# A four-layer graph network with expert layers on one core: sparse routers that work on raw rows, and moved pieces at the start of two block loops

## The chip, the core and the metric

One core of a Trainium2 chip runs the whole program in one launch. The metric is the device time in microseconds (us). The kernel before takes 1663.86 us, the median of 3 runs (1663.5 to 1666.35).

## What is computed

Rows x (625 nodes by 512 features, f32) go through eight steps, each `x = x + step(layernorm(x))`: four graph layers (GNN) and, after each, a layer of 8 experts. In layers 1 and 3 the expert layer is sparse: each row goes to its two best experts alone.

```python
x = x + _L1_ffn_ref(_layernorm(x, axis=-1)[None], gate_w, gate_b, w1, b1, w2, b2)[0]

# layer 1                                          # layer 3
logits = x @ gate_w + gate_b                       logits = x @ router_w.T
topk_vals, topk_idx = top_k(logits, 2)             probs = softmax(logits)
weights = softmax(topk_vals), one-hot to experts   gates, idx = top_k(probs, 2); gates = gates / sum(gates)
h = relu(x @ w1[e] + b1[e])                        h = silu(x @ w1[e].T) * (x @ wgate[e].T)
out = sum_e (h @ w2[e] + b2[e]) * weights[:, e]    out = sum_e combine[:, e] * (h @ w2[e].T)
```

The layer norm has no gains: `(x - mean) / sqrt(var + 1e-5)`. The expert layers 0 and 2 are dense (every expert for every row).

## The kernel before, in words

**Layout.** The 625 rows lie in 5 tiles of 125 rows (`X`, T = 5). `XN` is the normalised copy, `XT` its transpose (512 features in 4 groups of 128 partitions by 625 rows). Each engine has its own program in the file (PE's begins near L768, ACT's near L1500, DVE's near L1935, POOL's near L585, SP's near L555); they meet through semaphores, and each engine goes through its own list strictly in order. So what stands where in a list is the schedule.

**The sparse layer.** A router r (1 or 3) finds for each row two experts. The rows are counted per expert, each expert's rows get whole blocks of 128 slots, 17 blocks in all, and PE works through the blocks. For each block it needs the 128 rows turned (`xblk`, then `xbh` and `xbl`, a rounded value and the rest) and the weights of the block's expert, in a rounded part ("high", written by ACT, L1627) and a rest ("low", written by DVE, L384). Each product is three passes: high by high (L1075), rest by high (L1076), high by rest (L1079).

**Router before, as each engine runs it.** DVE: `normalise` writes XN (L2003), `feats` copies the transposes to XT (L1950), `low` makes the first weights' rest (L384), then `router(r)` (L2106 to L2159): logits, maximum, exp (ACT L1568), sum, quotient `PR`, the 8 sorted values and indices (L2135, L2138), the mask `MK` of the two chosen (L2146), and the weights `COMB` (L2152 to L2159). PE: `routed_feats` turns XN (L779), multiplies XT by the gate matrix (L800, 16 instructions), waits for ACT's copy of the logits, turns them into rows (L958). `slots` on PE (L1039) counts the mask with 12 narrow products and waits for COMB; `slots` on DVE (L2183 to L2205) gives the slot of each row and the two-hot tiles `SEL0`. With `SEL0` PE picks the first block's rows in 40 products (`chosen_nodes`, L1116), so that block 0 needs no transfer; POOL meanwhile scatters all rows of XN to DRAM (`scatter`, L688) for the later blocks.

**Start of the block loop before (`block_loop`, `body1`).** In layer 1 PE turns COMB (L1056), adds the second biases of rows 0 and 1 (L1061, 4 instructions) ahead of block 0's nodes, then runs the first product of block 0, the other biases (L1053), the second product, block 1's nodes by `SEL1` (L1116 again), and `turn(0)` (L1101). DVE at this place: xbl (L2268), the rest of weights a1, `blocks_of` (which expert has which block, L2213 to L2225, on which SP waits for the loads of block 1; then the kept weights and block biases, L2228 to L2237), `second_rows` (SEL1, L2242 to L2248), `second_biases` (L2256), the hidden copy (L2280), the rest of weights y0, and xbl of block 1 (L2268).

**keep(b, n)** is n products of constants (L790, two instructions each) whose result nobody reads; they occupy PE while it would wait.

## Time and profile before

| | us |
|---|---|
| median of 3 runs | 1663.86 |
| the profiled execution | 1662.77, span 1660.0 |
| PE busy | 1586.0 (96%) |
| DVE busy | 1243.7 (75%) |
| ACT busy | 935.0 (56%) |
| POOL busy | 292.2 (18%) |
| mean granted TensorE clock | 0.987 of full |

The page gives each engine's busy time, the span in 40 slices of 41.5 us, the chain of work that ended last, and the costliest groups of instructions. PE is on 79% of that chain and DVE on 14%. The two routers lie at 686 to 734 us and 1159 to 1205 us; the block loops behind them run to about 945 and 1645 us.

### The profile page before, as it was taken

What the parts mean: (1) busy time and instruction counts of PE and PEld (TensorE: products, weight loads), DVE (VectorE), ACT (ScalarE), POOL (GpSimd) and SP (SyncE); (2) the same over time, 40 slices, a digit from 0 to 9 for tenths busy, and PEclk for the clock granted to TensorE, in tenths of its full rate; (3) what the DMA queues carried; (4) which work ended last, traced back from release to release, by engine and by line L of the source; (5) the groups of instructions that cost most, each with busy time, mean ns of one, the idle gap of its engine ahead of it and who ended that gap; (6) DMA issues with size and microseconds to landing.
All of it is one profiled execution on the core that took longest, in us unless ns stands there. A gap on an engine that the chain in (4) does not pass through costs nothing.

```text
span 1660.0 us, 26245 instructions
## 1 busy us (share of the span) xinstructions
PE 1586.0 (96%) x8681; PEld 1243.7 (75%) x8681; DVE 1243.7 (75%) x2138; ACT 935.0 (56%) x1572; POOL 292.2 (18%) x276
## 2 busy tenths in 40 slices
PE   9997998999999999889999999999899999999998
PEld 8885765868877886477788765865588888888886
DVE  8836663464756575879999868553799999999997
ACT  1423463443634462249999653421388787787884
POOL 0023730010210121179000302000470000000003
PEclk9998999999999999989999999999999999999999
DMA  8010000022001002054952340005253438935003
GB/s 337 20 46 6 1 2 14 1 115 77 2 3 37 1 2 102 26 171 151 325 207 93 89 159 1 1 1 228 54 221 138 169 127 358 387 141 219 25 19 99
DMA packets 42239, 173.14 MB, mean 104 GB/s; under 512 B 10219, under 2 KB 10472, under 8 KB 26681
## 3 DMA queue, kind: packets, MB, share of 16 engines
q1 hardware_dynamic: 28742, 153.75, 24.2%
q0 software_dynamic: 8960, 10.29, 2.3%
q10 hardware_dynamic: 4464, 8.13, 1.3%
q8 instruction: 46, 0.75, 0.2%
q14 instruction: 27, 0.22, 0.0%
HBM read 275.54 MB, written 19.25 MB: 178 GB/s over the span
## 4 chain that ended last, share of the span: by engine, by line
PE 79%; DVE 14%; issue 2%; ACT 2%; POOL 1%; DMA 1%; DVEq 0%; SPq 0%; ACTq 0%; POOLq 0%
PE bank L1075 10%; PE bank L1079 10%; PE bank L1076 10%; PE bank L927 4%; PE bank L899 4%; PE bank L974 3%; PE bank L887 3%; PE bank L839 3%; PE bank L1023 3%; PE bank L1199 3%; PE bank L1307 3%; PE bank L858 2%; PE bank L1369 2%; PE bank L1101 2%; PE bank L1281 2%
## 5 line engine op out<-in xcount | busy, mean ns | idle before, releaser
L715 POOL DMA_INDIRECT sb_W<-slots_out,sb_slus x20 | 29.9, 1494 | 541.3 <-DMA slots_out<-sb_rC 535.8
L1530 ACT ACTIVATE sb_rF<-sb_rF,sb_nmx 125x625 f32<-125x625 f32 (+4 forms) x120 | 89.5, 746 | 45.0 <-DVE sb_nmx L2072 44.9
L653 POOL TENSOR_TENSOR sb_rstd<-sb_ve,sb_half 125x3 f32<-125x3 f32 (+4 forms) x29 | 25.4, 876 | 442.7 <-DVE sb_ve L1976 238.1
L790 PE MATMUL bank<-sb_ones 128*128 128x512 f32 x208 | 95.5, 606 | 3.8 <-DVE sb_rC L2625 1.3
L384 DVE TENSOR_TENSOR sb_rA_r<-sb_W,sb_rA_r 128x1024 fp32r<-128x1024 f32 x68 | 83.6, 1229 | 12.2 <-ACT sb_rA_r L1627 12.0
L2072 DVE CUSTOM_DVE_ANT_0 sb_rF<-bank,sb_rG 125x625 f32<-125x625 f32 x80 | 61.5, 807 | 36.1 <-PE bank L887 35.2
L384 DVE TENSOR_TENSOR sb_XT_r<-sb_W,sb_XT_r 128x1024 fp32r<-128x1024 f32 x68 | 83.3, 1226 | 0.0
L384 DVE TENSOR_TENSOR sb_rB_r<-sb_W,sb_rB_r 128x1024 fp32r<-128x1024 f32 x68 | 83.2, 1224 | 0.0
L1627 ACT ACTIVATE sb_rA_r<-sb_W 128x1024 fp32r<-128x1024 f32 x68 | 71.5, 1052 | 19.5 <-DMA sb_W<-in_w_m 15.8
L1662 ACT ACTIVATE sb_rG_r<-bank 128x512 fp32r<-128x512 f32 x51 | 30.6, 600 | 82.3 <-PE bank L1101 82.3
L790 PEld LDWEIGHTS bank<-sb_ones 128*128 128x128 f32 x208 | 39.0, 193 | 47.9 <-issue 44.5
L927 PE MATMUL bank<-sb_rA,sb_rDE 125*64 125x125 f32 x1040 | 69.0, 275 | 4.5 <-DVE sb_rA L2086 4.3
L899 PE MATMUL bank<-sb_ident,sb_rF 125*125 125x125 f32 x520 | 69.7, 279 | 3.0 <-DVE sb_nmx L2072 3.0
L1627 ACT ACTIVATE sb_XT_r<-sb_W 128x1024 fp32r<-128x1024 f32 x68 | 71.6, 1053 | 0.0
L1627 ACT ACTIVATE sb_rG_r<-sb_W 128x1024 fp32r<-128x1024 f32 x68 | 71.6, 1053 | 0.0
L1627 ACT ACTIVATE sb_rB_r<-sb_W 128x1024 fp32r<-128x1024 f32 x68 | 71.3, 1049 | 0.3 <-PE bank L1079 0.3
L927 PEld LDWEIGHTS bank<-sb_rA,sb_rDE 125*64 125x64 f32 x1040 | 54.8, 136 | 20.6 <-DVE sb_rA L2086 13.0
L899 PEld LDWEIGHTS bank<-sb_ident,sb_rF 125*125 125x125 f32 x520 | 61.3, 188 | 9.0 <-issue 6.8
L384 DVE TENSOR_TENSOR sb_AT_r<-sb_W,sb_rG_r 128x1024 fp32r<-128x1024 f32 x51 | 62.0, 1216 | 0.0
L2086 DVE COPY sb_rA<-bank 125x500 f32<-125x500 f32 (+3 forms) x60 | 37.6, 627 | 30.7 <-PE bank L899 30.6
L1075 PE MATMUL bank<-sb_XT_r,sb_rC_r 128*128 128x512 f32 x136 | 59.3, 436 | 0.0
L1075 PE MATMUL bank<-sb_rA_r,sb_rC_r 128*128 128x512 f32 x136 | 53.6, 394 | 4.4 <-ACT sb_rC_r L1641 3.9
(534 smaller groups left out, 4783.5 us busy)
## 6 DMA issues: line engine op xcount, KB each, us to landing
sb_W<-in_w_m SPq DMA_DIRECT2D x204, 1024.0 KB
sb_rDE<-in_w_m SPq DMA_DIRECT2D x17, 1024.0 KB
sb_rC<-slots_in SPq DMA_DIRECT2D x33, 256.0 KB, 2.7
sb_W<-in_w_g SPq DMA_DIRECT2D x8, 1024.0 KB, 4.9
slots_out<-sb_rC ACTq DMA_DIRECT2D x31, 256.0 KB, 2.0
slots_in<-sb_rC SPq DMA_DIRECT2D x1, 4608.0 KB, 24.7
sb_W<-in_w_a SPq DMA_DIRECT2D x4, 1024.0 KB, 17.1
sb_W<-in_w_m SPq DMA_DIRECT2D x2, 2048.0 KB, 16.8
```

The source lines that it names most:

```text
L384: eng.tensor_tensor(lo, src[:, HALF * h:HALF * (h + 1)], hi.bitcast(F32), ALU.subtract).then_inc(split(r, p, h, b, "lo")[0], 1)
L790: pe.matmul(bank[:, b, :], ones[:], ones[:, 0:1].broadcast_to([P, D]), start=True, stop=True)
L839: mm = pe.matmul(bank[:, j, 0:hi - lo], w[:, c, m * P:(m + 1) * P], x[:, c, lo:hi], start=(n == 0), stop=(n == len(steps) - 1))
L887: mm = pe.matmul(bank[0:R, b, at:at + n], q[hp, h // 2, t * R:(t + 1) * R], keys, start=(i == 0), stop=(i == len(terms) - 1))
L899: return pe.transpose(bank[0:R, b, at:at + R], SM[:, (2 * p + a) % 4, kb * R:(kb + 1) * R], ident[0:R, 0:R])
L927: mm = pe.matmul(bank[a * DH:(a + 1) * DH, 6 + g % 2, p % 2 * R:(p % 2 + 1) * R], V[:, kb, h + a, :], PT[:, p % 2, 8 + a if kb == 4 else 4 ...
L1075: pe.matmul(dst, high[2 * h + k], w_hi[:, k], start=(opens and h == 0 and k == 0), stop=False)
L1076: pe.matmul(dst, low[2 * h + k], w_hi[:, k], start=False, stop=False)
L1079: mm = pe.matmul(dst, high[2 * h + k], w_lo[:, k], start=False, stop=(closes and h == 1 and k == 1))
L1530: act.activation(SM[:, s % 4, 0:kn], SM[:, s % 4, 0:kn], ACT.Exp, scale=-1.0, bias=nmx[:, s:s + 1], accum_out=dens[:, s:s + 1]).then_inc(S ...
L1627: act.activation(half(r, p, h)[0], part(PLACE[r][p])[:, HALF * h:HALF * (h + 1)], ACT.Copy).then_inc(split(r, p, h, b, "hi")[0], 1)
L2072: dve.tensor_tensor_reduce(out=SM[:, s % 4, 0:kn], in0=scores, in1=mask(t), scale=-1.0, scalar=3e38, op0=ALU.add, op1=ALU.min, accum_out=n ...
```

## The change

- **Router on raw rows.** `raw_gates` turns the raw rows X as soon as each tile is final, ACT copies each tile to XT (`raw_tiles`), and PE multiplies the tile by the gate columns straight into rows. `picks` on DVE corrects for the mean (mean times the gate columns' sum, `gsum`) and multiplies by 1/sqrt(var). The 8 sorted values come from the logits; the mask MK is done before exp and the weights, and PE's `slots` waits for the mask alone. `gsum` is made once, inside router 0: 8 narrow products on PE and one copy on DVE.
- **XN** is written by ACT (`normal_rows`), after the mask.
- **Fewer constant products.** keep(7, 17) becomes keep(7, 10) ahead of router 1, keep(7, 6) ahead of router 3 goes, the routers' keep(5, 4) becomes keep(5, 3), and two keep(5, 3) stand around `slots` and the turning of COMB in layer 1.
- **Moved pieces.** COMB is turned in `turn_weights`, ahead of the block loop; biases 0 and 1 come after block 0's nodes; the nodes of block 0 go tile by tile as SEL0 is written; block 1's nodes come ahead of the product a1; `second_rows` comes ahead of the rest of a1 on DVE; the rest of weights a0 comes after `slots`; `blocks_of` runs ahead of the block loop, and the kept weights and block biases become `kept_weights` at the old place.

```diff
+            def raw_gates(r, ready, base):
+                for t in range(T + 1):
+                    if t < T:
+                        pe.wait_ge(ready, base + t + 1)
+                        for c in range(C):
+                            mm = pe.transpose(bank[:, t, c * R:(c + 1) * R], X[:, t, c * P:(c + 1) * P], ident[0:R, 0:R])
+                        mm.then_inc(S("tr_full"), 1)
+                    if t >= 1:
+                        u = t - 1
+                        pe.wait_ge(S("x0"), ROWS_XT[r] + u + 1)
+                        for c in range(C):
+                            mm = pe.matmul(bank[0:R, 7, u * E:(u + 1) * E], XT[:, c, u * R:(u + 1) * R], gw[:, c, GW[r]:GW[r] + E],
+                                           start=(c == 0), stop=(c == C - 1))
+                mm.then_inc(S("rt_pe"), 1)
...
-                pe.wait_ge(S("rt_vec"), ROUTED[r] + ROUTER_OPS[r])
+                pe.wait_ge(S("rt_vec"), ROUTED[r] + PICKED[r])
...
+                if c == 3:
+                    for k in range(C):
+                        pe.matmul(bank[0:R, 2, 0:32], ones[:, 0:R], gw[:, k, 0:32], start=(k == 0), stop=(k == C - 1))
...
-            keep(7, 17)
-            routed_feats(4, 5, 1)
-            feats_ready(5)
+            keep(7, 10)
+            raw_gates(1, S("lf_vec"), LF_OPS)
+            keep(5, 3)
             slots(1)
-            second_biases(0, 2)
+            turn_weights()
+            keep(5, 3)
             block_loop(1)
...
-            keep(7, 6)
-            routed_feats(8, 9, 3)
-            feats_ready(9)
+            raw_gates(3, S("rows_vec"), 3 * T)
+            keep(5, 3)
             slots(3)
             keep(5, 4)
             block_loop(3)
...
                         second_biases(2, T)
-                        first("a", 1, b)
                         pe.wait_ge(S("rows_off"), 2 * T + 1)
                         pe.wait_ge(S("b_xbl"), 1)
                         chosen_nodes(lambda t: SEL1[t])
+                        first("a", 1, b)
...
-                pe.wait_ge(S("sl_vec"), SLOT_OPS * (r // 2) + SELECTED)
-                chosen_nodes(lambda t: SEL0[:, t])
+                pe.wait_ge(S("x0"), ROWS_XN[r] + T)
+                chosen_nodes(lambda t: SEL0[:, t], True)
+                if r == 1:
+                    pe.wait_ge(S("rt_act"), RT_ACT[1] + 3)
+                    pe.wait_ge(S("ld_b2"), 64)
+                    second_biases(0, 2)
...
+            def raw_tiles(r):
+                for t in range(T):
+                    act.wait_ge(S("tr_full"), T * (5 if r == 1 else 9) + t + 1)
+                    act.activation(XT[:, :, t * R:(t + 1) * R], bank[:, t, 0:C * R]..., ACT.Copy).then_inc(S("x0"), 1)
+            def normal_rows(r):
+                act.wait_ge(S("ln_vec"), LN[4 if r == 1 else 8] + STATS + 1)
+                for t in range(T):
+                    act.activation(XN[:, t], X[:, t], ACT.Identity, scale=rstd[...], bias=shift0[...]).then_inc(S("x0"), 1)
...
+            def picks(r):
+                c(dve.tensor_tensor(EX[:], means, gsum[...], ALU.mult))
+                dve.wait_ge(S("rt_pe"), RT_PE[r] + 1)
+                c(dve.tensor_tensor(LG[:], bank[0:R, 7, 0:T * E]..., EX[:], ALU.subtract))
+                dve.wait_ge(S("pow"), POW[f"ln{k}"])
+                c(dve.tensor_tensor(LG[:], LG[:], bcast(rstd[0:R, :], E), ALU.mult))
+                dve.scalar_tensor_tensor(out=shift0[:], ...).then_inc(S("ln_vec"), 1)
+                if r == 1:
+                    c(dve.tensor_tensor(LG[:], LG[:], rbias[...], ALU.add))
+                for t in range(T): c(dve.max(m8[:, t], LG[:, t]))
+                for t in range(T): c(dve.max_index(i8[:, t], m8[:, t], LG[:, t]))
+                c(dve.tensor_copy(if8[:], i8[:]))
+                for k in range(2):
+                    c(dve.tensor_tensor(EQ[:, k], iota8..., if8[:, :, k:k + 1]..., ALU.is_equal))
+                c(dve.tensor_tensor(MK[:], EQ[:, 0], EQ[:, 1], ALU.add))
+                assert c.n == ROUTED[r] + PICKED[r]
+                c(dve.tensor_tensor(LG[:], LG[:], m8[:, :, 0:1]..., ALU.subtract))
+                dve.wait_ge(S("rt_act"), RT_ACT[r] + 1)
+                c(dve.tensor_tensor(COMB[:], EX[:], MK[:], ALU.mult))
+                c(dve.tensor_reduce(red[:, 2], COMB[:], AX.X, ALU.add))
+                c(dve.reciprocal(red[:, 2], red[:, 2]))
+                c(dve.tensor_tensor(COMB[:], COMB[:], bcast(red[:, 2], E), ALU.mult))
...
-            normalise(n, 4, X)
-            feats(5, XT)
+            picks(1)
+            slots(1)
             low(dve, 1, ("a", 0), 0, part(PLACE[1]["a", 0]))
-            router(1)
-            slots(1)
+            blocks_of(1)
...
-                    lows(("a", 1), b)
                     if before is None:
-                        blocks_of(1)
                         second_rows()
+                    lows(("a", 1), b)
+                    if before is None:
+                        kept_weights(1)
                         second_biases()
```

## Rows read from the trace of the kernel before

**Rows 1.** The page's part 2: granted TensorE clock in tenths, 40 slices.
```profile
PEclk9998999999999999989999999999999999999999
```
**Rows 2.** Chain that ended last, layer 1's router: start, duration, engine, output, line, count.
```profile
683.41 0.65 DVE sb_X L2661
...
699.63 1.48 PE bank L1039 x12
...
702.47 3.77 PE bank L1061 x4
...
706.24 7.59 PE bank L1116 x40
```
**Rows 3.** PE's timeline there: start, duration, line; in brackets idle before and releaser.
```profile
670.26 14.82 PE L790 MATMUL bank<-sb_ones 128*128 128x512 f32 x34
...
686.24 2.47 PE L779 MATMUL bank<-sb_ident,sb_XN 125*128 125x125 f32 x20 [1.16 <-DVE sb_XN L2003]
...
715.27 0.47 PE L1075 MATMUL bank<-sb_rA_r,sb_rC_r 128*128 128x512 f32 x1 [1.46 <-ACT sb_rC_r L1641]
...
718.20 2.83 PE L1053 MATMUL bank<-sb_b,sb_rF 8*125 8x512 f32 x6
...
725.80 1.97 PE L1116 MATMUL bank<-sb_rA,sb_XN 125*128 125x128 f32 x8 [1.80 <-DVE sb_rB L2248]
...
733.62 0.47 PE L1075 MATMUL bank<-sb_rA_r,sb_rC_r 128*128 128x512 f32 x1 [1.02 <-ACT sb_rC_r L1641]
```
**Rows 4.** DVE's timeline, the same stretch.
```profile
696.51 0.44 DVE L2135 MAX8 sb_m<-sb_LG 125x8 f32<-125x8 f32 x5
...
698.37 0.20 DVE L2146 TENSOR_TENSOR sb_MK<-sb_EQ 125x40 f32<-125x40 f32 x1
...
704.31 1.40 DVE L2205 SCALAR_TENSOR_TENSOR sb_W<-sb_iotaP,sb_sl,sb_W 125x128 f32<-125x128 f32 x5
...
717.36 0.16 DVE L2213 TENSOR_TENSOR sb_nblk<-sb_nblk 128x8 f32<-128x8 f32 x1
...
719.05 0.24 DVE L2228 TENSOR_REDUCE sb_wk<-sb_rDE 125x10 f32<-125x80 f32 x1
...
730.59 1.22 DVE L384 TENSOR_TENSOR sb_W_r<-sb_W,sb_rDE_r 128x1024 fp32r<-128x1024 f32 x1
```
**Rows 5.** Timelines of ACT, POOL and SP's queue, the same stretch.
```profile
687.38 0.59 ACT L1513 ACTIVATE sb_XT<-bank 128x500 f32<-128x500 f32 x1 [18.41 <-PE bank L779]
...
730.01 1.06 ACT L1627 ACTIVATE sb_rA_r<-sb_W 128x1024 fp32r<-128x1024 f32 x1 [13.67 <-DMA sb_W<-in_w_m]
...
704.41 1.58 POOL L688 DMA_INDIRECT slots_in<-sb_XN,sb_slu  x1 [17.67 <-issue]
...
722.24 1.18 SPq L502 DMA_DIRECT2D sb_W<-in_w_m  x2
```
**Rows 6.** Stretches: length, busy PE, PEld, DVE, ACT, POOL; granted clock, DMA share, GB/s.
```profile
703.00:706.00 3.00, 3.00 (x4) 0.65 (x2) 2.64 (x12) 1.31 (x2) 1.58 (x1) 0.50 0.01 3
...
726.00:727.00 1.00, 1.00 (x6) 1.00 (x6) 1.00 (x3) 0.00 (x0) 0.00 (x0) 0.50 0.94 393
```
**Rows 7.** PE's and DVE's timelines, layer 3's router and the block loop's start.
```profile
1164.76 0.67 DVE L2057 TENSOR_TENSOR sb_X<-bank,sb_X 125x512 f32<-125x512 f32 x1
...
1180.53 0.38 PE L1039 MATMUL bank<-sb_MK,sb_TRI 125*125 125x40 f32 x2 [1.16 <-DVE sb_COMB L2159]
...
1186.66 4.73 PE L1116 MATMUL bank<-sb_W,sb_XN 125*128 125x128 f32 x40 [1.14 <-DVE sb_W L2205]
...
1192.85 0.47 PE L1075 MATMUL bank<-sb_rA_r,sb_rC_r 128*128 128x512 f32 x1 [1.46 <-ACT sb_rC_r L1641]
...
1205.18 0.47 PE L1075 MATMUL bank<-sb_AT_r,sb_rG_r 128*128 128x512 f32 x1 [0.64 <-issue]
```
**Rows 8.** PE's timeline, router 0's logits.
```profile
275.90 4.44 PE L1347 MATMUL bank<-sb_rC,sb_gw 128*64 128x375 f32 x16
```
**Rows 9.** A stretch of the first block loop, columns as in rows 6.
```profile
740.00:750.00 10.00, 10.00 (x50) 8.21 (x49) 10.00 (x13) 9.67 (x15) 10.00 (x6) 1.00 0.45 157
```

145 lines of the change are left out of this document (84 added, 61 removed).

## Prediction

> **What bounds the kernel now.** I read four views in this order. The page's engine table and slices first: PE is busy in nearly every slice and holds a full clock nearly everywhere [rows 1], so time can only come out of places where PE waits or runs slowly. Then the chain of work that ended last around each sparse router: it leaves PE there and walks through DVE and ACT operations of 0.2 us [rows 2]. Then the timelines of PE and DVE in those two places, for the waits and what ends them [rows 3, 4, 7]. Last a stretch of the block loop behind: PE and DVE are both busy for all of 10 us [rows 9]. The loop moves as one piece, so what is saved ahead of it is kept, if DVE, ACT and the loads reach it in the old order.
>
> **Router 1 up to the mask.** Before: the last tile of X is final at 683.41 + 0.65 = 684.06 [rows 2], and the narrow counting products start at 699.63 [rows 2], 15.6 us later. After: four transposes of the last tile cost 4/20 of 2.47 = 0.49 us [rows 3]. ACT's copy of it costs 0.59 [rows 5]. The tile's logits are 8 narrow instructions; the nearest row is L1039, 12 in 1.48 us, 0.12 each [rows 2], so 0.99 a tile. Tile 3's logits stand behind tile 4's transposes and cover the copy, so the logits end at 684.06 + 0.49 + 2 x 0.99 = 686.5, with a hand-over 686.6. That assumes keep(7, 10) is over: 17 constants took 14.82 us from 670.26 [rows 3], 0.87 each, so ten end at 679.0, before the first tile.
>
> DVE then has four short operations (subtract, scale, shift0, bias), 0.23 each (0.20 for the mask's own operation [rows 4] and a hand-over), and the known piece from the first MAX8 to the mask's end, 698.57 - 696.51 = 2.06 [rows 4]. The mask is there at 686.6 + 0.92 + 2.06 = 689.6. The new keep(5, 3), 2.6 us, ends before it. The counting starts at 689.7 instead of 699.63: **9.9 us**. Exp, the sum and the weights lie beside the counting's 1.48 us.
>
> **Router 1 up to block 0's first product.** DVE's slot chain depends on the counting and shifts by 9.9. SEL0's last five operations started at 704.31 and took 1.40 [rows 4]; PE may now start at the first of the five, 704.31 + 0.28 - 9.9 = 694.7. Counting, turning and keep(5, 3) end at 689.7 + 1.5 + 0.6 + 2.6 = 694.4. The 40 products took 7.59 us here [rows 2] and 4.73 in layer 3 [rows 7]. In the first case they followed four bias products of 0.94 each [rows 2] in a stretch with a granted clock of 0.50 [rows 6]; at the full clock six such cost 2.83, 0.47 each [rows 3]. With constants ahead I take 4.73: nodes end at 699.4. The four bias instructions now follow (1.9 us) and hide the 1.46 us wait for xbh and xbl [rows 3]. Block 0's first product starts at 701.3 instead of 715.27: **14.0 us**.
>
> **From there to block 1's first product.** Before this took 733.62 - 715.27 = 18.35 us [rows 3], with PE waiting 1.80 us for SEL1 and then at half clock [rows 3, 6]. PE's new list would need 2.9 + 2.8 + 4.6 + 2.8 + 0.5 = 13.6. DVE is the later one: its old list ended with y0's rest at 730.59 + 1.22 = 731.8, 16.5 us after the first product; blocks_of, 719.05 - 717.36 = 1.7, has left it [rows 4], so 14.8. Xbl and the hand-overs are 1.46 less ACT's 0.59, 0.9 [rows 3, 5]: 15.7. So block 1 begins at 717.0 and the gain is 733.62 - 717.0 = **16.6 us**. What is late next is DVE's list; PE idles some 2 us ahead of block 1.
>
> **What is moved past other queues.** SP waits for blocks_of, which now ends near 700 instead of 719.05, so its two loads for block 1 go out near 703 instead of 722.24 [rows 5]. ACT got them at 730.01, 7.8 us later [rows 5]; that would be 711. They now share the DMA engines with POOL's ten scatters, which began at 704.41 [rows 5] and now begin near 694.5, so the loads can land as late as 714.5. ACT's two copies, xbh and xbl behind them need 3.6 us, so block 1 starts between 714.6 and 718.1: the cost is 0 to 1.1, and I take 0. Had the loads not moved, they would land at 730 and nearly all of the 2.7 us and more would be lost; this cover carries much. On ACT, the first copies of a0 end near 687.5, exp runs at 690, five XN rows at 0.59 [rows 5] end at 693.1, 1.6 us before PE wants them; if a row cost 1.06, the largest ACT piece [rows 5], it would be 0.7 late. The scatter needs XN too and is 9.9 earlier at best. On DVE the rest of a0 (2.3) and blocks_of (1.7) stand between SEL0 (695.8) and xbl (700.1): they end at 699.8, so they are free by 0.3.
>
> **Router 3.** The last X ends at 1164.76 + 0.67 = 1165.43 [rows 7]; plus 0.49 + 1.98 + 0.1 is 1168.0; three short operations and 2.06 give the mask at 1170.7, and the counting starts at 1170.8 instead of 1180.53 [rows 7]: 9.7. The nodes start at the first SEL0 tile, another 4/5 of 1.40 = 1.1 earlier. DVE has 1.7 less in the loop's first round, which should take away PE's wait of 0.64 at 1205.18 [rows 7]. Sum **11.4 us**. The 1.46 wait at 1192.85 stays [rows 7].
>
> **Router 0 pays.** gsum is 8 narrow instructions, 8 x 0.12 = 0.99, ahead of the last quarter of a group that ran without a gap (16 in 4.44 us) [rows 8], plus a DVE copy of 0.23 on the same path: **-1.2 us**. Bounds: 0 if PE was to wait there, 1.2.
>
> **The clock.** Between keep(7, 10) and keep(5, 3) PE has 7.5 us in which it does short transposes and 8-column products with gaps, in layer 3 the same for 8.3 us. The rows show what went before a half clock: narrow products with gaps at 699.6 to 702.5 went before the 0.50 of 703 to 706 [rows 2, 6], and an idle of 1.80 us before the 0.50 at 726 [rows 3, 6]. Against it, 20 transposes in 2.47 us went before a full clock [rows 3]. The change's stretches look more like the first. Price at half clock, by L1116's 7.59 against 4.73 and the biases' 0.94 against 0.47: transposes and logits +1.5, keep 2.6 more, of which 0.5 is hidden, +2.1; if it goes on, counting and turning +1.2, second keep +2.3, nodes +2.9. The bounds are 0 and 10.0 in layer 1, 0 and 9.5 in layer 3. I take the first two terms, 3.6 for each router since constants, which keep PE busy without a gap, stand right behind.
>
> The Trainium skill ("TensorE: Matmul & The Clock Gate", "What's actually happening") says that "the default state is throttled, and activity releases the throttle"; that speaks against taking constants away, and it is the second rival's rule. The same page ("Wait — 56ns, not 53.3ns?") gives about 62 ns of sequencer time for a small matmul without hardware decoding. By that, an estimate, a tile's logits would cost 0.5 and each router would come 1 us earlier, 2 in all; the narrow row here has 0.12 an instruction, and the sum goes by it.
>
> **Sum.** 16.6 + 11.4 - 1.2 = 26.8 at full clock; less 2 x 3.6 = 19.6. The profiled execution has 1662.77 (span 1660.0, 2.8 around it): 1662.77 - 19.6 = **1643.2**. The median of the runs is 1.1 above the profiled one, inside the range.
>
> **Rivals.** (1) *The clock stays full in both routers*: 1662.77 - 26.8 = 1636.0. For it: narrow work keeps PE occupied, and the 20 transposes. Against it: the half clock after 699.6 to 702.5. (2) *Half clock carries on to the nodes in both*: 26.8 - 10.0 - 9.5 = 7.3, so 1655.5. For it: the 7.59 us of the old nodes; against it: constants now stand on both sides of the counting. (3) *The change doesn't do what it says*: the mask is early, but XN or the weights of COMB end last, and only the moved pieces count, 16.6 - 9.9 + 1.7 - 1.2 = 7.2, so 1655.6. Little speaks for it; XN has 1.6 us to spare. (4) *Slower: the block loop settles in another order*. PE and DVE are both full [rows 9]; if block 1 enters with DVE late and each of the 31 later blocks (15 and 16) keeps PE waiting once for xbl, by the 1.02 us seen at 733.62 [rows 3], that is 31.6, so 1643.2 + 31.6 = 1674.8. It decides from 19.6/31 = 0.63 us a block. Against it: all but the first round's order is unchanged, and at 740 to 750 PE had no gap although 733.62 began with one.
>
> **How the numbers follow.** Forecast 0.60, rival (1) 0.18, (2) 0.12, (3) 0.04, (4) 0.04, and 0.02 that smaller losses meet at no change. Range 1634.5 to 1652.0: it takes in (1) with 1.5 for the loads and row 8's bound, and on the upper side 8.8 for a half clock that carries on in one of the two routers; it leaves out (2), (3), (4) and the rest, 0.2 at most. Faster by over 0.2% (3.3 us, about what a measurement of this kernel can tell from no change): 0.60 + 0.18 + 0.12 + 0.04 = 0.94; same 0.02; slower 0.04.
>
> **What would show it.** In the changed kernel's PE timeline: 20 narrow groups between 679 and 687 (all 1 us later for router 0), counting 15.6 - 9.9 = 5.7 us after the last X; nodes of block 0 in about 4.8 us and biases right behind; the wait ahead of block 1's first product ended by DVE's xbl, some 2 us; ACT's first copy of block 1 not later than 714.5. In layer 3 counting 5.4 us after the last X. The granted clock between each router's last X and its counting decides between the forecast, (1) and (2). The prediction is wrong if the counting is later than 8 us after the last X, if ACT's wait for block 1's load ends last, or if a block's round in either loop has become longer.

## The result, and the profile after

| | us |
|---|---|
| changed kernel, median of 5 runs | 1653.34 (1647.62 to 1655.17) |
| before, median of 5 runs beside it | 1663.86 (1661.35 to 1666.35) |
| ratio | 0.9932, 95% interval 0.9917 to 0.9946 |
| its profiled execution | 1647.62, span 1645.4, mean granted clock 0.983 |
| DVE, PE busy | 1233.9, 1580.1 |

The change gains 10.5 us. The forecast was 20.7 below the median of before and its range ended at 1652.0, so it was wrong: the sign is right, but half of the gain is missing. The profiled execution is the quickest of the five. The other four have granted clocks of 0.980 to 0.982.

PE's timeline around router 1 and the start of the first block loop (start, duration, line, tiles; in brackets the idle time before it and what ended it). It answers to [rows 3] and the PE steps of [rows 2].

```profile
687.92 0.65 PE L828 MATMUL bank<-sb_ident,sb_X 125*128 125x125 f32 x4
688.40 2.07 PE L834 MATMUL bank<-sb_gw,sb_XT 128*125 128x8 f32 x16
690.33 4.33 PE L794 MATMUL bank<-sb_ones 128*128 128x512 f32 x6
694.49 0.31 PE L1059 MATMUL bank<-sb_MK,sb_TRI 125*125 125x40 f32 x2
...
699.61 4.59 PE L1136 MATMUL bank<-sb_W,sb_XN 125*128 125x128 f32 x39 [0.59 <-DVE sb_W L2277]
...
706.15 0.50 PE L1093 MATMUL bank<-sb_rA_r,sb_rC_r 128*128 128x512 f32 x1
...
721.42 0.47 PE L1093 MATMUL bank<-sb_rA_r,sb_rC_r 128*128 128x512 f32 x1 [1.59 <-issue]
...
728.28 0.60 PE L1144 MATMUL bank<-sb_ident,sb_rC 128*128 128x128 f32 x4
...
736.64 0.49 PE L1093 MATMUL bank<-sb_rA_r,sb_rC_r 128*128 128x512 f32 x1 [1.76 <-DVE sb_rC_r L2344]
...
744.66 0.60 PE L1144 MATMUL bank<-sb_ident,sb_rC 128*128 128x128 f32 x4
```

DVE there: the last tile of X, and the mask (answers to [rows 4]).

```profile
687.12 0.75 DVE L2738 SCALAR_TENSOR_TENSOR sb_X<-sb_XN,sb_rstd,sb_X 125x512 f32<-125x512 f32 x1
...
693.14 0.20 DVE L2232 TENSOR_TENSOR sb_MK<-sb_EQ 125x40 f32<-125x40 f32 x1
```

The last X is final at 687.87, 3.8 us later than before: that much was lost upstream. From there it goes better than forecast. The counting (L1059) begins 6.6 us after the last X where before had 15.6, the nodes (L1136) run at the full clock in 4.7 (all 40), and block 1's first product (721.42) begins 33.6 us after the last X where before had 733.62 - 684.06 = 49.6 [rows 2, 3]: 16.0 us gained. Then a new loss. L1144 turns block 2's nodes at 728.28 and block 3's at 744.66. I call that distance block 2's round: 16.4 us, and 12.38 before (740.65 to 753.03). PE's wait of 1.76 us is in it, and right behind the wait a stretch at half clock, which costs some 1.7 us more (start:end, length, busy PE, PEld, DVE, ACT, POOL, then granted clock, DMA share, GB/s):

```profile
738.00:741.00 3.00, 2.92 (x7) 2.35 (x8) 3.00 (x5) 3.00 (x5) 3.00 (x2) 0.50 0.23 87
```

What the other engines did there (answers to [rows 5]): ACT's waits for DMAs, SP's DMA issues, and two of POOL's ten scatter pieces.

```profile
716.00 1.06 ACT L1670 ACTIVATE sb_rA_r<-sb_W 128x1024 fp32r<-128x1024 f32 x1 [9.16 <-DMA sb_W<-in_w_m]
724.53 1.06 ACT L1670 ACTIVATE sb_W_r<-sb_W 128x1024 fp32r<-128x1024 f32 x1 [0.85 <-DMA slots_in<-sb_XN,sb_slu]
731.18 2.02 ACT L1670 ACTIVATE sb_rDE_r<-sb_W 128x1024 fp32r<-128x1024 f32 x2 [2.94 <-DMA sb_W<-in_w_m]
```

```profile
707.73 3.60 SPq L506 DMA_DIRECT2D sb_W<-in_w_m  x2
724.52 0.34 SPq L511 DMA_DIRECT2D sb_rC<-slots_in  x1
725.15 5.58 SPq L506 DMA_DIRECT2D sb_W<-in_w_m  x4
```

```profile
708.83 2.95 POOL L692 DMA_INDIRECT slots_in<-sb_XN,sb_slu  x1 [0.30 <-issue]
...
717.59 1.19 POOL L692 DMA_INDIRECT slots_in<-sb_XN,sb_slu  x1 [0.30 <-issue]
```

Read them together. POOL's last scatter piece ends at 718.8; at 724.5 SP's and ACT's waits for the scatter end together. SP could not issue block 1's y0 load before that, since the wait and the node load (724.52) stand ahead of it on its queue. The load goes out at 725.15 and is in use at 731.18; ACT idles 2.94 us, and xbh, xbl and PE's first product of block 2 come late behind it. Before, POOL's scatter had ended 13 us ahead of block 1's first product; now it ends 2.6 ahead.

Router 3, with one line each of DVE, PE and ACT (answers to [rows 7]):

```profile
1155.81 0.68 DVE L2097 TENSOR_TENSOR sb_X<-bank,sb_X 125x512 f32<-125x512 f32 x1
```

```profile
1157.03 2.86 PE L834 MATMUL bank<-sb_gw,sb_XT 128*125 128x8 f32 x16
1159.73 5.13 PE L794 MATMUL bank<-sb_ones 128*128 128x512 f32 x6
1164.70 0.31 PE L1059 MATMUL bank<-sb_MK,sb_TRI 125*125 125x40 f32 x2
...
1169.82 4.70 PE L1136 MATMUL bank<-sb_W,sb_XN 125*128 125x128 f32 x40 [0.18 <-DVE sb_W L2277]
1175.98 0.47 PE L1093 MATMUL bank<-sb_rA_r,sb_rC_r 128*128 128x512 f32 x1 [1.46 <-ACT sb_rC_r L1684]
```

```profile
1193.87 1.06 ACT L1670 ACTIVATE sb_XN_r<-sb_W 128x1024 fp32r<-128x1024 f32 x1 [3.37 <-DMA slots_in<-sb_XN,sb_slu]
```

The counting begins 1164.70 - 1156.49 = 8.2 us after the last X (before 15.1), the first product 19.5 after it (before 27.4): 7.9 gained. The six constant passes, 2.75 us at the full clock, took 5.13. Ahead of y1's copy ACT now waits 3.37 us for the scatter; the second loop's first round (between the first two L1144) takes 28.1 instead of 26.6.

Stretches with the granted clock as third number from the end, first of the changed kernel, then of before (answers to [rows 6]):

```profile
284.00:287.00 3.00, 3.00 (x12) 2.92 (x11) 1.95 (x4) 0.75 (x2) 0.00 (x0) 0.50 0.00 0
482.00:485.00 3.00, 3.00 (x6) 1.56 (x6) 0.00 (x0) 0.00 (x0) 0.00 (x0) 0.50 0.00 0
...
1158.00:1164.00 6.00, 6.00 (x14) 3.56 (x15) 3.24 (x27) 4.33 (x6) 0.48 (x1) 0.50 0.01 1
```

```profile
284.00:287.00 3.00, 2.83 (x18) 2.54 (x17) 2.06 (x5) 1.37 (x4) 0.00 (x0) 1.00 0.03 5
292.00:295.00 3.00, 2.62 (x9) 2.65 (x10) 1.50 (x4) 2.22 (x4) 0.00 (x0) 0.58 0.00 0
482.00:485.00 3.00, 3.00 (x14) 2.33 (x13) 1.53 (x3) 0.00 (x0) 0.00 (x0) 1.00 0.00 0
```

The changed kernel has half-clock stretches (1.2 GHz instead of 2.4) where before had none, two of them far ahead of the routers. Before is not free of them: it has, among others, one at 292 to 296 us, which the changed kernel has at 294 to 298, and in router 1 two more (702 to 713 and 725 to 730). Summed over windows of 1 us, one minus the granted clock comes to 1.7 us for each, or to two or three times that. From 100 to 1640 us this makes 25.6 us in the changed kernel's trace and 20.5 in before's.

The books of the two profiled executions, as the distance of the changed kernel's PE from before's:

| place | before | after | distance |
|---|---|---|---|
| router 0's second products | 296.75 | 298.56 | +1.8 |
| turn to rows ahead of router 1 | 667.52 | 671.32 | +3.8 |
| block 1's first product, layer 1 | 733.62 | 721.42 | -12.2 |
| turn of block 2's nodes | 740.65 | 728.28 | -12.4 |
| turn of block 3's nodes | 753.03 | 744.66 | -8.4 |
| last turn of that loop | 929.95 | 919.53 | -10.4 |
| turn to rows ahead of router 3 | 1156.91 | 1147.95 | -9.0 |
| block 0's first product, layer 3 | 1192.85 | 1175.98 | -16.9 |
| turn of block 2's nodes there | 1240.60 | 1225.23 | -15.4 |
| turn of block 15's | 1586.66 | 1572.07 | -14.6 |

### The profile page after: what moved, and what is told of

It reads as the page before. It is cut to its first block, busy times and chain, and to the rows that moved or that the text cites. A ratio compares the mean times of both kernels' runs of the same rounds, so it can differ in the third digit from the quotient of the medians.

```text
span 1645.4 us, 26288 instructions
## 1 busy us (share of the span) xinstructions
PE 1580.1 (96%) x8703; PEld 1246.9 (76%) x8703; DVE 1233.9 (75%) x2122; ACT 942.8 (57%) x1584; POOL 293.5 (18%) x276
## 4 chain that ended last, share of the span: by engine, by line
PE 80%; DVE 12%; issue 3%; ACT 2%; DMA 1%; POOL 1%; DVEq 0%; SPq 0%; ACTq 0%; POOLq 0%
PE bank L1097 10%; PE bank L1093 10%; PE bank L1094 10%; PE bank L947 4%; PE bank L919 4%; PE bank L994 4%; PE bank L907 3%; PE bank L859 3%; PE bank L1043 3%; PE bank L1331 3%; PE bank L1223 3%; PE bank L878 2%; PE bank L1396 2%; PE bank L1119 2%; PE bank L1305 2%
## 5 line engine op out<-in xcount | busy, mean ns | idle before, releaser
L794 PE MATMUL bank<-sb_ones 128*128 128x512 f32 x184 | 88.5, 628 | 3.8 <-DVE sb_rC L2702 1.3
L1670 ACT ACTIVATE sb_XT_r<-sb_W 128x1024 fp32r<-128x1024 f32 x68 | 71.7, 1055 | 0.0
L1670 ACT ACTIVATE sb_rB_r<-sb_W 128x1024 fp32r<-128x1024 f32 x68 | 71.4, 1050 | 0.2 <-PE bank L1097 0.2
## 6 DMA issues: line engine op xcount, KB each, us to landing
sb_W<-in_w_m SPq DMA_DIRECT2D x2, 2048.0 KB, 16.9
```

Source lines behind the costliest of these rows:

```text
L794: pe.matmul(bank[:, b, :], ones[:], ones[:, 0:1].broadcast_to([P, D]), start=True, stop=True)
L1670: act.activation(half(r, p, h)[0], part(PLACE[r][p])[:, HALF * h:HALF * (h + 1)], ACT.Copy).then_inc(split(r, p, h, b, "hi")[0], 1)
```

## Experiments

The theory that I formed from these traces (S): the routers' part of the forecast holds; the missing gain is in the scatter, which has become late, in the sums' place in router 0, and in half-clock stretches.

**The changed kernel again.** No edit.

> The changed kernel again, unchanged. Theory S (the scatter of the first routed layer has become late, and half-clock stretches fall at other places each time): 1651 to 1655 us as a median, and the executions stay some 7 us apart with the granted clock (0.980 to 0.983). In its trace block 2 of the first loop again takes 16.4 us after block 1 where before had 12.4, and the first round of the second loop 28.1 where before had 26.6, while the half-clock stretches of the middle of the kernel need not be where they were. Rival L (a late load was an accident of the one profiled execution): block 2's round is 12.4 to 12.9 and the median comes out near 1650.

Measured: 1653.24 us (1649.31 to 1654.51), ratio 0.9928 (0.9912 to 0.9944). Block 2's round is 14.8 us, again with ACT waiting for y0 (2.49 us); the second loop's first round is 27.2. The difference to 16.4 is the half clock behind PE's wait, which this trace lacks:

```profile
738.00:741.00 3.00, 2.56 (x13) 1.87 (x12) 3.00 (x4) 3.00 (x5) 3.00 (x2) 1.00 0.23 87
```

The loss is a property of the kernel, its size is not: theory S holds with smaller numbers, rival L falls. In router 3 the half clock lies at 1158 to 1169 us and costs 5.1 instead of 3.4.

**Before, again.** No edit.

> The kernel before, unchanged, for a second trace of it. Question: are the half-clock stretches that only the changed kernel's four traces have ahead of its first routed layer (284 to 288 us in all of them, 481 to 486 in three) a property of the change or of the execution? Theory C (the stretches fall by chance; any kernel may get them): this trace has one at 284 to 288 us or at 481 to 486 us too, or its landmarks ahead of router 1 lie 1 to 3 us from those of the first trace of before. Theory P (the change brings them, in router 0 by the sums of the gate weights and the order around them): no such stretch, the start of router 0's second products at 296.5 to 297.0 us and the turn to rows ahead of router 1 at 667.5 within 0.5 us.

Measured: 1663.92 us, ratio 0.9998 (0.9985 to 1.0011). Ahead of router 1 its stretches are those of the first trace of before and the turn to rows is at 668.04, 0.5 later: P. Router 0's second products start at 297.23, outside the range expected, but 20.9 us after the logits' start (276.37) as in the first trace. Behind it two more stretches came (1050 to 1055 and 1170 to 1174 us) and its end lies 3.9 us behind the first trace's, so far down one kernel differs from itself by whole microseconds.

**The y0 load ahead of the scatter's wait.**

```
                 weights(("a", 1), 1, e, new)
+                weights(("y", 0), 1, e, new)
                 sp.wait_ge(S("sc"), 16 * 2 * T * (r // 2 + 1))
                 nodes(2)
-                weights(("y", 0), 1, e, new)
```

> The changed kernel with one load moved on SP's queue: the y0 weights of block 1 of the first loop go ahead of SP's wait for the scatter and of the node load of block 2, which were ahead of them. Theory S: VectorE is done with these weights' place at 720.7 us, the scatter's wait kept SP until 724.5, and the load landed at 731.2 with ScalarE idle 2.9 us for it; issued at 721 it lands by 728, ScalarE's wait of 2.9 us goes, VectorE's 1.5 and TensorE's 1.8 after it too, and block 2's round falls from 16.4 to 12.4 to 13.6 us. The median falls by 2 to 4 us to 1650 (half clock at 737 to 741 us, which followed TensorE's pause, may go as well). Rival D (the load is slow because the scatter's packets share the DMA engines, not because it is issued late): it lands at 730 or later all the same and the round stays above 15 us, the median within 1 us of the changed kernel's.

Measured: 1651.88 us (ratio 0.9923, 0.9908 to 0.9938). SP's issues and PE's turns of nodes:

```profile
708.84 13.52 SPq L506 DMA_DIRECT2D sb_W<-in_w_m  x3
725.62 0.34 SPq L511 DMA_DIRECT2D sb_rC<-slots_in  x1
```

```profile
730.09 0.66 PE L1144 MATMUL bank<-sb_ident,sb_rC 128*128 128x128 f32 x4 [0.60 <-DMA sb_rC<-slots_in]
...
742.55 0.60 PE L1144 MATMUL bank<-sb_ident,sb_rC 128*128 128x128 f32 x4
```

Three loads are out by 722.4 instead of two, ACT waits no more for y0, and block 2's round is 12.46, with block 1's first product 33.6 us after the last X as in the changed kernel: the mechanism is as theory S said, and rival D falls. Now PE waits 0.60 us for the node load. The median moved by 1.4 us, less than the 2 to 4 expected and within what the intervals leave open. Over the whole loop, from block 2's turn to the last turn, this trace takes 190.0 us, and the two of the changed kernel 191.3 and 192.8 (before 189.3): there the edit is worth 1.2 and 2.8.

**Half the scatter.** The rows of each node's second expert are not scattered, and who waits for the scatter waits for that half.

```
-                for k in range(2):
+                for k in range(1):
                     for t in range(T):
                         pool.indirect_dma_start(out=XS, ...
```

> The changed kernel with only half of each scatter: the first expert's rows of each token go to the slots, those of the second are left out (5 of 10 indirect DMAs), and who waits for the scatter waits for that half. Theory S: POOL is done near 709 instead of 718.8 us, no wait of SP or ScalarE ends with the scatter; block 2's round in the first loop 12.4 to 13.4 us instead of 16.4, the second loop's first round 26.6 to 27.0 instead of 28.1; the median 4 to 6 us under the changed kernel's, 1647 to 1649. Rival O (the first rounds are longer because of the new order of nodes, products and blocks ahead of the loop): both rounds stay, and the median stays within 1.5 us.

Measured: 1649.25 us, ratio 0.9904 (0.9887 to 0.9921), 4.1 below the changed kernel. No wait of ACT or SP ends with the scatter; block 2's round 12.7, the second loop's first round 26.7. Taken alone this trace doesn't show that the scatter is the cause, for half clock in router 1 (688 to 695 and 711 to 719 us) made block 1's first product late, 38.0 us after the last X instead of 33.6. With the full scatter and as late a start (two constants, below: 37.9) the rounds are 12.4 and 26.7 as well, and with the sums left out (36.3) block 2's is 12.5. A block that starts that much later no longer waits for the load. And rival O falls by these traces, which have the new order and rounds as short as before's.

**The moved pieces alone.** The kernel before, with the moved pieces (turned copy, biases, nodes by tile, SEL1 ahead, blocks counted ahead), the keep(5, 3) ahead of block 0's nodes, and its own routers.

> The kernel before with the moved pieces alone: turned copy of the weights and biases 0 and 1 at their new places, block 0's nodes tile by tile, block 1's nodes ahead of the second part of block 0's first products, blocks counted ahead of the loop; the routers stay on normalised rows. By the forecast's terms: router 1 gives 14.0 - 9.9 = 4.1 us to block 0's first product and 16.6 - 14.0 = 2.6 more to block 1's, router 3 10.8 - 9.7 = 1.1 and its wait of 0.64; together 8.4, so 1655 to 1657 us against a median of 1664 to 1666 of before. Theory S (the lateness of the scatter, which ran to 720 us in before, is met only where all parts come together): block 2's round in the first loop stays at 12.4 to 13. Rival O (the new order itself makes block 2's round longer): it is 14 us or more, and the gain only 4 to 6 us. Theory N on the 0.06 us that every round of the second loop lost: if a moved piece brings it, the rounds are 26.68 here, otherwise 26.62.

Measured: 1656.27 us, ratio 0.9959 (0.9945 to 0.9973), 7.5 us gained. Block 0's nodes and block 1's first product:

```profile
704.66 4.73 PE L1115 MATMUL bank<-sb_W,sb_XN 125*128 125x128 f32 x40 [0.48 <-DVE sb_W L2208]
...
726.49 0.47 PE L1072 MATMUL bank<-sb_rA_r,sb_rC_r 128*128 128x512 f32 x1 [1.58 <-issue]
```

Block 0's first product comes 4.0 us earlier (forecast 4.1), block 1's 7.1 (forecast 6.7), router 3 adds 1.0 (forecast 1.1; its 0.64 not). Block 2's round is 12.5, with the scatter over 4.1 us ahead of block 1's first product. The terms for the moves were right, and alone they meet no late scatter. A part of this gain is clock: router 1's half clock of before (702 to 713 and 725 to 730 us) isn't in this trace, and the mean granted clock of the seven executions is 0.986 to 0.991.

**The sums alone.** The kernel before with the eight products and the copy.

```
             for c in range(C):
+                if c == 3:
+                    for k in range(C):
+                        pe.matmul(bank[0:R, 2, 0:32], ones[:, 0:R], gw[:, k, 0:32], ...)
                 pe.wait_ge(S("wo0_done"), 2 * c + 2)
```

> The kernel before with the sums of the gate weights alone (eight products ahead of the last chunk of router 0's logits, and the copy on VectorE; nothing uses them). The changed kernel's traces lie 1.8 to 3.4 us behind before at router 0's second products and 2.7 to 4.8 us at the turn to rows ahead of router 1, the one without the sums 1.4 and 1.8. Theory U (the sums and what follows from them are that whole delay): router 0's second products 1.8 to 2.7 us later, with a half-clock stretch at 284 to 288 us, the turn to rows 2 to 4 us later, and the median 2 to 4 us above before's. Theory A (the sums cost their own time, and the stretches came otherwise): 1.0 to 1.3 us later at both places, no stretch at 284 to 288, median 1 us above before's, 1664.5 to 1665.5.

Measured: 1668.54 us against 1663.75, ratio 1.0030 (1.0019 to 1.0042): 3.2 to 7.0 us slower. PE in router 0:

```profile
278.48 1.06 PE L1348 MATMUL bank<-sb_gw,sb_ones 128*125 128x32 f32 x8
...
283.88 1.23 PE L989 MATMUL bank<-sb_ident,sb_W 125*72 125x125 f32 x5 [1.98 <-DVE sb_W L2132]
```

The products take their 1.06 us, and behind the pause the transposes take 1.23 where before had 0.70: the granted clock of 284 to 287 is 0.50, and 1.00 in before. But before's own stretch of 292 to 296 us is gone in exchange:

```profile
292.00:295.00 3.00, 1.68 (x9) 1.30 (x9) 1.89 (x5) 2.82 (x6) 0.00 (x0) 1.00 0.00 0
```

From the logits' start to the second products it is 22.1 us against 20.9: 1.25 more, which is the forecast's 1.2 and no clock on top. So theory U's numbers did not come (second products 0.5 us later instead of 1.8 to 2.7, turn to rows 0.9 instead of 2 to 4), nor did theory A's, since the stretch is there. The medians say 4 times the forecast's cost, and the one trace doesn't show where: it is 2.3 us ahead of before at the first loop's last turn (927.66 against 929.95) and 2.6 behind at the end, of which 0.8 are the second loop's rounds of 26.68. It was also one of the two quickest of twelve executions.

**The sums left out.** The changed kernel without the eight products and the copy; the logits then lack the correction for the mean.

> The changed kernel without the eight products and the copy that sum the gate weights in router 0 (left out: the sums, which are zero here, so the tokens' means are not taken out of the logits of routers 1 and 3). Theory S with its upstream part U (the 1.06 us of products ahead of router 0's last logits start a pause and a half-clock stretch there): router 0's mixture starts 2 us earlier, at 292.4 as before the change, and the half clock at 284 to 287 us goes; the median falls by 1.5 to 3 us, to 1650 to 1652. Rival (half clock in router 0 comes and goes by itself): the start of the mixture moves by 0.7 us at most, and the median by under 1 us.

Measured: 1651.89 us, ratio 0.9915 (0.9895 to 0.9934). Router 0's second products start at 298.17, 0.4 to 1.2 us earlier than in the changed kernel's two traces, and 22.2 us after the logits' start instead of 23.5. The half clock of 284 to 288 is there all the same. Neither side was right: the products' own time goes, the stretch stays. In the changed kernel the sums thus cost 1.3 us in the trace and 1.4 in the medians of the same session, with intervals that overlap.

**Two constants instead of three.**

```
             raw_gates(1, S("lf_vec"), LF_OPS)
-            keep(5, 3)
+            keep(5, 2)
```

and the same in router 3.

> The changed kernel with two constant products instead of three between the logits and the counting, in both sparse routers. Theory K (where the clock is at half, the three constants outlast VectorE's choice: the counting began 1.15 us after the mask in router 1 and 2.2 us after it in router 3): the counting begins 0.15 to 0.9 us after the mask in both; 1 us gained in router 1 and 1.5 us in router 3, median 1650 to 1652. Rival (fewer constants leave the clock at half for longer, and block 0's nodes take 7 us instead of 4.7): nothing gained or 1 to 2 us lost.

Measured: 1652.42 us, ratio 0.9932 (0.9916 to 0.9948): nothing gained. Router 3:

```profile
1165.07 3.76 PE L794 MATMUL bank<-sb_ones 128*128 128x512 f32 x4
...
1168.91 2.31 PE L1059 MATMUL bank<-sb_MK,sb_ones 125*125 125x32 f32 x10
1171.02 5.06 PE L794 MATMUL bank<-sb_ones 128*128 128x512 f32 x8
```

The counting is nearer to the mask, 0.5 and 0.8 us behind it, as expected. But the clock stays at half longer: the ten counting products take 2.31 us and the eight constant passes 5.06, which were 1.27 and 3.69, and from the counting to the first product it is 13.2 us in router 1 and 13.4 in router 3 instead of 11.7 and 11.3. The nodes themselves are at the full clock. What the shorter queue gives, the clock takes. In all six executions the mean granted clock is 0.977 to 0.980, in the eleven of the changed kernel 0.980 to 0.983. Three constants are no guarantee either: with half the scatter, where they stand as in the changed kernel, router 3 has half clock from 1155 to 1170 us.

**Constants between the tiles of router 3.**

```
                     if t < T:
+                        if r == 3 and 1 <= t <= 3:
+                            keep(5, 1)
                         pe.wait_ge(ready, base + t + 1)
```

> The changed kernel with one constant product ahead of the turns of row tiles 1, 2 and 3 in router 3, where TensorE waited 0.4 to 0.7 us for each tile. Theory H (the pauses and 8-column products there bring the half clock of 1157 to 1169 us, which costs 3.4 to 5.1 us of TensorE's time, of it 2 to 3 on the path): no half-clock stretch between 1150 us and block 0's first product, logits 2.5 to 3 us after the last row tile instead of 3.2 to 5.6, counting 5.5 to 6.2 us after it instead of 8.4 to 10.1; the median 1.5 to 3 us lower, 1650 to 1651. Rival (the products push the turns back by as much): the logits' end moves by under 0.5 us, and the median stays.

Measured: 1649.08 us, ratio 0.9913 (0.9898 to 0.9927), 4.3 below the changed kernel, or 3.2 by the ratios, whose intervals overlap a little. PE, and the stretch with its granted clock:

```profile
1163.37 2.83 PE L794 MATMUL bank<-sb_ones 128*128 128x512 f32 x6
1166.20 0.41 PE L1061 MATMUL bank<-sb_MK,sb_TRI 125*125 125x40 f32 x2
```

```profile
1150.00:1170.00 20.00, 19.58 (x114) 13.76 (x113) 12.74 (x55) 10.74 (x16) 1.55 (x2) 1.00 0.00 0
```

With the last X at 1160.01 the counting begins 6.2 us after it instead of 8.2 and 9.4 (the two traces of the changed kernel), right behind the mask (1166.14). The logits end 3.5 us after the last X (without the edit 3.4 and 5.4): against the first trace the products push the tiles back as much as the clock gives. The gain is in the constants behind them, 2.83 us instead of 5.13. Theory H holds, with more in the constants than in the logits. The first product of block 0 comes 17.6 us after the last X instead of 19.5 and 20.7, and the six executions have a mean granted clock of 0.983 to 0.988. The same edit stands in the three kernels below; two of their traces have no half clock in router 3, the last one has it again from 1161 to 1165 us.

**Three edits together.** The y0 load ahead, the constants in router 3, and the sums behind the last chunk of router 0's logits instead of ahead of it.

> The changed kernel with three edits: the y0 load of block 1 ahead of the scatter's wait, one constant product ahead of the turns of tiles 1 to 3 in router 3, and the sums of the gate weights after the last chunk of router 0's logits, where TensorE waits 0.46 us for ScalarE, instead of ahead of it. If the findings add up: block 2's round 12.4 to 12.9 (before it 16.4 and 14.8), no half clock in router 3, and 0.4 to 1.1 us less in router 0 (the sums' 1.1 us against a pause of 0.46, the logits' end stays behind them); the median 1646 to 1649. Against it: if the gains are only the chance places of half clock, it stays at 1649 to 1653 like the kernels with one edit.

Measured: 1644.01 us (1640.65 to 1646.68), ratio 0.9885 (0.9866 to 0.9903), clear of the changed kernel's interval and 2 us below what was expected. Router 0 and the turns of nodes:

```profile
280.71 1.06 PE L1377 MATMUL bank<-sb_gw,sb_ones 128*125 128x32 f32 x8
281.70 0.70 PE L980 MATMUL bank<-sb_ident,sb_rF 8*125 8x8 f32 x5
284.39 0.70 PE L1010 MATMUL bank<-sb_ident,sb_W 125*72 125x125 f32 x5 [1.99 <-DVE sb_W L2166]
...
727.26 0.60 PE L1146 MATMUL bank<-sb_ident,sb_rC 128*128 128x128 f32 x4
...
739.70 0.60 PE L1146 MATMUL bank<-sb_ident,sb_rC 128*128 128x128 f32 x4
```

The sums now fill the pause of 0.46 us, the transposes take 0.70 as in before, there is no half clock between 263 and 685 us, and the turn to rows is at 667.46 instead of 671.32. Block 2's round is 12.44. By the medians 9.3 of the 10.1 us between the changed kernel and the forecast are back, but not all of it by the three edits. In router 0 this trace is 3.5 us shorter than the changed kernel's (20.0 from the logits' start against 23.5), and 3.4 of that are two half-clock stretches that it lacks, one of them (292 to 296) a stretch that before had too; the next kernel but one has the sums at the same place and both stretches again, at 22.9. And router 1 runs worse than in the changed kernel: half clock from 685 to 693 us, counting 8.2 us after the last X instead of 6.6, block 1's first product 36.3 instead of 33.6. So between the turn to rows and the turn of block 3's nodes only 1.1 us is left of the 3.9 that block 2's round gave; router 3 gives 1.9.

**Constants in both routers.** The same, with the products ahead of tiles 1 to 3 in router 1 too.

> The kernel with the three edits, and the constant products ahead of the turns of tiles 1 to 3 in router 1 too, where TensorE did not wait for the tiles. Theory B (there TensorE is the one that is late: each product pushes the turns back by its 0.92 us, and only the clock comes back): logits end 1 to 2.5 us later after the last row tile, the constants after them run at full clock and are 1.6 us shorter, so counting within 1 us of the same and the median the same within 1.5 us, 1647 to 1650. Rival (the clock is worth more than the products anywhere): counting 1 us earlier, the half clock at 690 to 694 us gone, and the median 1 to 3 us lower than with three edits.

Measured: 1645.84 us, ratio 0.9890 (0.9871 to 0.9908). The logits end 4.3 us after the last X (with three edits 3.1), the counting begins 8.5 after it (8.2), and a stretch at 688 to 692 us stays. The constants behind the logits became 0.95 us shorter, not 1.6. Theory B in the main: where PE itself is the late one, constants bought nothing here.

**The sums' buffer at the end.** Three edits, and the 128 bytes declared behind the big buffers.

> The kernel with the three edits, and the buffer of the gate weights' sums (128 bytes of each partition) declared after all other buffers instead of ahead of the weights' and rows' buffers, which it moved up by 128 bytes. Every round of the second loop took 26.62 us in the three kernels without this buffer or the one that is not moved by it (before twice, the moved pieces alone), and 26.67 to 26.68 in all that have it ahead of the others, the one that leaves the sums out and the one of before with the sums among them. Theory P (the place of the big buffers makes the difference): the rounds are 26.62 here, 0.9 us less over fifteen of them, median 1642 to 1645. Rival (something else of these programs does it): 26.67 or more. The half clock of the routers may fall otherwise and move the whole by 2 us.

Measured: 1644.67 us, ratio 0.9882 (0.9866 to 0.9899). A round of the second loop, here and in the changed kernel:

```profile
1331.56 0.60 PE L1146 MATMUL bank<-sb_ident,sb_rC 128*128 128x128 f32 x4
...
1358.17 0.60 PE L1146 MATMUL bank<-sb_ident,sb_rC 128*128 128x128 f32 x4
```

```profile
1331.95 0.60 PE L1144 MATMUL bank<-sb_ident,sb_rC 128*128 128x128 f32 x4
...
1358.63 0.60 PE L1144 MATMUL bank<-sb_ident,sb_rC 128*128 128x128 f32 x4
```

26.61 and 26.63 in turn, against 26.68: theory P. The first loop's rounds are 12.37 instead of 12.41 as well. That is some 1.4 us over both loops, below what the medians resolve (0.7 us apart the other way). The stretches at 284 and 294 us came back in this trace, with the sums at the later place, and so did one in router 3, with the constants between the tiles.

## Why the prediction was wrong

Two of the three signs that it named came: the counting of router 3 began more than 8 us after the last X, and rounds of both loops became longer. The step that failed is the overlap in "What is moved past other queues": it followed SP's queue as far as the loads of a0 and took the cost as 0, and the next load behind them, y0, was late behind the scatter. Two further terms were wrong: half clock outside the routers was put at nothing, and one profiled execution stood for the kernel.

By the two profiled spans the gain is 14.6 us (1660.0 - 1645.4), 5.0 less than the 19.6 of the forecast. By the books above: 2.6 were lost ahead of router 1 (3.8 instead of 1.2), 3.0 more than forecast were gained in router 1, 0.2 gained in block 1, 4.0 lost in block 2's round, 2.0 regained in the rest of the loop, 1.4 lost between the loop and router 3, 0.7 more than forecast gained in router 3, 2.1 lost in the second loop's first round (1.5 lost instead of 0.64 gained), and 0.8 in its other rounds. The range was missed by 1.3 us; with either the y0 load moved (1651.88) or the constants in router 3 (1649.08) the median lies inside it. Point by point:

**The mask and the slots: right.** The narrow products cost 0.12 us each at the full clock (eight in 0.94), as taken from the counting's row. The forecast with its half clock had the counting 5.7 + 3.6 = 9.3 us after router 1's last X and 5.4 + 3.6 = 9.0 after router 3's; measured 6.6 and 8.2.

**Nodes, biases, SEL1: right.** 4.70 us for the nodes in both routers against 4.73; block 1's first product 15.3 us after block 0's against 15.7, with DVE's xbl (720.64) ahead of it. Up to that product 16.0 us were gained from the last X against 16.6 - 3.6 = 13.0, in router 3 7.9 against 10.8 - 3.6 = 7.2. Here the forecast was 3.7 us too low. That holds for these executions: in the traces where router 1 had more half clock (half the scatter, the sums left out, two constants, and the three kernels with three edits) block 1's first product comes 36.3 to 38.2 us after the last X instead of 33.6, a gain of 11.4 to 13.3.

**"What is moved past other queues": failed.** I followed SP's two loads of block 1 and asked when a0 would land (forecast 711 to 714.5, measured 716.0, and PE waited for DVE all the same). I stopped there. Behind these two SP waits for the scatter, and the y0 load stands behind that wait. The scatter had been 13 us early; block 1's first product moved 12.2 us forward, the scatter's start only 5.2 (704.41 to 699.21: 9.0 gained up to the slots, less 3.8 for the late X) and its end 1.6, for it took 19.6 us instead of 16. This last comes with DVE's large two-input operations: a piece of 1.19 us took 2.95 (708.83) beside the rest of weights a1 (708.37 to 710.7), in which DVE reads two operands of 1024 columns from SBUF, and 1.19 (714.60 to 717.6) beside additions that have one operand in a bank; before, the one long piece (2.10 at 715.27) lay beside the same weights. The Trainium skill ("SBUF — State Buffer", "SBUF: two separate sides") says that a DVE operation with two SBUF inputs and a GpSimd operation that reads SBUF take a shared port pair as an exclusive lock, for the whole instruction. The trace agrees in these pieces, as far as times side by side can show it; a piece at 1179.87 took 1.19 us beside the same kind of operation. Cost of the late y0 load: 4.0 us of block 2's round in the traced execution, of which some 1.7 are the half clock behind the wait, and 2.4 in the repeat; in the second loop, where y1's copy waits for the scatter itself, 1.5 and 0.5, where I had entered a gain of 0.64. Not all of it stays: in the first trace 2.0 came back later in the first loop, where rounds 3 to 9 are 1.1 us longer in sum than the even rounds behind them; in before these are 3.8 longer, and in the repeat 4.3. Moving the load by itself gave 1.2 and 2.8 us over the loop, and 1.4 in the medians.

**"Router 0 pays 1.2": right in place, too little in the medians.** The sums' own time was right, 1.06 us, and so is the distance in router 0 (1.25 more than before in the timing of the sums alone, 1.3 in the changed kernel with and without them). What the forecast didn't have is the second half-clock stretch at 284 to 288 us, 1.7, which the changed kernel has there with the sums and without, and what 128 bytes ahead of the weights' buffers do to every round, some 1.4. By the medians the sums alone cost 4.8 us (3.2 to 7.0) in the kernel before; no trace shows where more than 2.6 of that lie.

**The clock: right in kind, wrong in place.** I charged 3.6 for each router and nothing elsewhere. In the first trace router 1 paid 1.7 and router 3 3.4, in the repeat 1.7 and 5.1, and against before a stretch more came at 284 and at 481, one behind PE's wait in block 2 and one at 1038 us. The Trainium skill ("TensorE: Matmul & The Clock Gate", "What's actually happening") has the rule that the default is throttled and activity releases it; two constants against three (mean granted clock 0.977 to 0.980 against 0.980 to 0.983) and constants between the tiles (0.983 to 0.988) agree with it in both directions. One trace with three constants had half clock from 1155 to 1170 us all the same. By it the second rival would have been 1655.5, which is nearer to the measured median than the forecast; but its mechanism, half clock through to the nodes, was not there: the nodes ran at the full clock in both routers.

**The base.** I worked from one profiled execution of before. The traced execution of the changed kernel gained 15.2 us on it (1662.77 - 1647.62), the medians 10.5: this kernel's executions spread over 5 to 8 us, and its trace was the quickest of five. The median lies 5.7 us above the trace in the changed kernel and 1.1 in before; the 4.6 between these are a part of the missing gain that no trace locates. The repeat's span is 4.2 us longer, in places: 0.9 at the turn to rows ahead of router 1, 2.4 at the first loop's last turn, 4.0 at the turn ahead of router 3.

**What stays open.** Why a stretch falls where it does. At 284 to 288 us all seven traces of the changed kernel's program with the sums in their first place or left out have one, and so does before with the sums; the two of before and the moved pieces alone do not; with the sums behind the logits two of three do not. The sums' time is not its only cause, since it stays without them. The stretch at 292 to 299 us is in before and the moved pieces alone, and in all these others but three: before with the sums, and the two with the sums behind the logits that lack the first one too. So neither is a plain price of the sums. Whether the stretches follow from what PE did just before, or from when it did it, no run here separates. Why a shift of 128 bytes slows some products of a round was not tried further. That the three edits give back 9.3 of 10.1 us in the medians is in part luck with the stretches in router 0.

## What to carry to other kernels

When a stretch ahead of a loop gets shorter, list for each queue and each engine what had slack there, down to the second and third wait, and subtract the gain from each slack: the scatter had 13 us and cost the loop a longer round when 2.6 were left, and none with 3.7 (the sums left out) or 4.1 (the moved pieces alone). Constant products paid where the engine waited for its input and bought nothing where it was the late one. Compare the granted clock of both kernels over the whole span before a delay is called the price of an edit: a half-clock stretch can also have moved. Here a small buffer was better placed behind the large ones, by 0.06 us in each round of the second loop.

## What the hardware showed that I had not expected

- 128 bytes ahead of the big buffers: rounds of 26.68 us instead of 26.62, and 12.41 instead of 12.37, in every trace that has them.
- The same PE instructions, started within 0.1 us of the same time (router 0 with the sums left out, and before), ran at half clock at 284 to 288 us in one kernel and at the full clock in the other: 22.2 against 20.9 us from the logits' start to the second products. Both had a further stretch some 10 us later.
- Two constants instead of three left the clock at half for 18 us with a granted mean of 0.53 (1156 to 1174), three more, spread between the tiles, kept it at 1.00 in three of four traces.
- A scatter piece: 1.19 us alone, up to 2.8 to 3.3 us beside some of DVE's operations with two operands of 1024 columns in SBUF; the last one counted as landed 5.7 us after POOL was done with it.
